# Loading the first section's weights first, and sending each token's residual with it to its expert

## The chip, the cores and the metric

The kernel runs on one core of a Trainium2 chip. A core has five engines that run their own instruction streams: TensorE (PE in the profile; PEld is its weight load), VectorE (DVE), ScalarE (ACT), GpSimd (POOL) and SyncE (SP), which here only issues transfers. Engines wait for one another and for transfers by semaphores. The metric is the device time of one execution in microseconds (us); lower is better.

## The reference, cut to what matters

The reference is a decoder of four layers with a self-attention part, a cross-attention part and a feed-forward part each, over 32 sequences of 128 tokens with 128 features (4,096 tokens). Each part normalizes the residual stream and adds its result to it. Only the last part matters for the change: a mixture of 8 experts in which every token goes to one expert.

```
h = layernorm(x)                          # 4096 x 128
e, p = argmax(h @ Wr), softmax value of it # one expert per token
place = number of earlier tokens that chose e   # dropped if place >= 512
y[token] = relu((p * h) @ W1[e]) @ W2[e]  # 128 -> 512 -> 128
out = x + y                               # dropped tokens: out = x
```

Everything ahead of it (a delta-rule layer first, then attention, gated and expert feed-forward layers, a state-space layer, L0_delta to L3_cross by the kernel's names) is computed section by section.

## The kernel before, in words

The 32 sequences are cut into groups of two (`G` = 2). Two streams of such groups, 0 and 1, are in work at once, half a round apart: while stream 0 is in its first six sections, stream 1 is in its last six, so that the engines find work in both. Strings of digits (`TURNS`, `LAST_TURNS`) say, for each engine, which stream issues its next piece; this order is fixed when the program is built. PSUM's eight banks are handed round as a ring (class `Psum`).

The program has these parts, with a barrier of all engines after each:

- Set-up (lines 461 to 528). SP and ACT issue the loads of the early weights, among them weights of later sections and constants that are staged in the streams' scratch memory. After all have landed, VectorE converts and scales (L505 to L522), and SP goes on issuing: the late weights (L471), the experts of L2_moe (L473, L477), and a transfer that writes zeros over `expert_in` in HBM (L480). The barrier waits for SP's issuing too.
- "first" (`stretch("first")`): stream 1 alone does its first six sections. Its inputs are loaded at the start (L2321 to L2324). VectorE's first piece waits for them. L0_cross waits for the late weights.
- "round", 7 times: both streams do twelve sections.
- "last": stream 0 does twelve sections, stream 1 its last six.
- The experts of L3_moe, in two rounds of 4 experts (L2462). SP loads for each expert its rows and both weights (L2528 to L2530). TensorE transposes the rows (L2470, 4 tiles of 128 tokens), multiplies up (L2475) and down (L2484). VectorE copies the result (L2522), and SP stores it to `expert_out` (L2533).
- The result, in two rounds of 16 sequences (L2548). SP loads places (L2552) and the stored residual (L2556), GpSimd gathers each token's row from `expert_out` with 16 indirect transfers (L2570), VectorE adds (L2583), SP stores `out` (L2561).

The function `moe3` (the section L3_moe inside the streams) only routes: the place of every token in `expert_in`, computed by short dependent VectorE operations, ending with L1356 (`place`) and L1358 (the row, scaled); GpSimd scatters the rows (L1367). SP's `stored` then stores the residual and the places to HBM (L2329, L2330), waits for these and the scatter, and loads the stream's next group (L2321).

## Time and profile before

| | us |
|---|---|
| median of 3 runs | 4756.86 |
| lowest and highest run | 4756.38, 4769.69 |
| profiled execution | 4767.48 |
| its span in the profile | 4765.8 |

| engine | busy, us | share |
|---|---|---|
| TensorE | 3863.3 | 81% |
| VectorE | 3144.0 | 66% |
| ScalarE | 2051.9 | 43% |
| GpSimd | 678.6 | 14% |

The profiled execution is as long as the longest of the three timed runs. Its span is the time from its first to its last recorded event. All times below count from the start of the span. By the timeline, "first" begins at 56 us, the experts of L3_moe at 4613 us and the result part at 4706 us.

### The profile page before, as it was taken

To read this page: it belongs to the slowest core of one execution; us is meant where nothing else is said; L and a number is where in the kernel's file an instruction comes from. 1 tells how busy PE (TensorE), PEld (TensorE's weight loads), DVE (VectorE), ACT (ScalarE), POOL (GpSimd) and SP (SyncE) were. 2 spreads that over 40 slices of the span, in tenths; PEclk is the share of its full clock that TensorE was granted. 3 is DMA by queue.
4 is the path that set the end of the run, shared out by engine and by line. 5 is a ranking of instruction groups with operands and counts; after the bars stand their busy time and mean duration, and the time that the engine had idled before them with its cause. 6 is when DMAs were issued, how large, how long until landed. Compare 5 with 4: busy or idle time off the path is not lost. (4 is left out here: it accounts for less than half of the span.)

```text
span 4765.8 us, 93107 instructions
## 1 busy us (share of the span) xinstructions
PE 3863.3 (81%) x36752; PEld 2707.5 (57%) x36752; DVE 3144.0 (66%) x8198; ACT 2051.9 (43%) x4873; POOL 678.6 (14%) x987
## 2 busy tenths in 40 slices
PE   1688888888878888788888888888888888889863
PEld 1456565655656565555656556565655656656642
DVE  3467767576765868677676767657686675765751
ACT  1236353454535454354534545353543535345520
POOL 1010201202020110202012020201102011120002
PEclk9679888798887988888888988879887897879886
DMA  4000000000000000000000000000000000000013
GB/s 130 1 2 1 7 2 7 2 1 7 1 7 1 6 2 1 8 1 7 2 7 2 1 7 1 7 1 6 2 1 8 1 6 2 6 2 1 1 35 91
DMA packets 69261, 45.67 MB, mean 10 GB/s; under 512 B 12995, under 2 KB 65852, under 8 KB 68590
## 3 DMA queue, kind: packets, MB, share of 16 engines
q1 hardware_dynamic: 63388, 33.03, 2.5%
q8 instruction: 303, 4.96, 0.4%
q0 software_dynamic: 2048, 3.85, 0.3%
q10 hardware_dynamic: 3378, 2.64, 0.3%
q14 instruction: 144, 1.18, 0.1%
HBM read 29.35 MB, written 10.50 MB: 8 GB/s over the span
## 5 line engine op out<-in xcount | busy, mean ns | idle before, releaser
L756 PE MATMUL banks<-scratch 32*128 32x512 f32 x2048 | 479.3, 741 | 45.3 <-DVE scratch L1741 17.6
L330 ACT ACT_TABLE_LOAD x321 | 411.8, 1283 | 13.3 <-PE banks L1083 7.8
L902 DVE TENSOR_REDUCE scratch<-banks 128x4 f32<-128x512 f32 x512 | 321.4, 681 | 76.8 <-PE banks L729 47.6
L1590 PE MATMUL banks<-scratch,w_ident 128*128 128x256 f32 x1024 | 298.8, 418 | 75.9 <-DVE scratch L1741 75.9
L1678 ACT ACTIVATE scratch<-scratch,ssm_A 128x256 f32<-128x256 f32 x512 | 231.4, 506 | 292.8 <-DVE scratch L1735 282.7
L866 ACT ACTIVATE scratch<-banks 128x512 f32<-128x512 f32 x512 | 269.9, 599 | 154.8 <-PE banks L790 154.1
L1874 PE MATMUL banks<-scratch 32*32 32x32 f32 x10496 | 274.0, 219 | 72.7 <-issue 44.8
L1735 DVE TENSOR_TENSOR_SCAN scratch<-scratch 128x512 f32<-128x512 f32 x256 | 312.9, 1222 | 15.4 <-ACT scratch L1678 8.6
L1874 PEld LDWEIGHTS banks<-scratch 32*32 32x32 f32 x10496 | 243.8, 131 | 123.4 <-issue 85.9
L581 POOL TENSOR_TENSOR 0_rstd<-0_var,minus_half 128x2 f32<-128x2 f32 x96 | 80.6, 840 | 1289.0 <-DVE 0_var L599 1079.3
L1590 PEld LDWEIGHTS banks<-scratch,w_ident 128*128 128x128 f32 x1024 | 191.9, 205 | 125.6 <-DVE scratch L1741 99.9
L806 PE MATMUL banks<-scratch 128*32 128x128 f32 x4096 | 225.1, 292 | 39.9 <-ACT scratch L866 31.0
L756 PEld LDWEIGHTS banks<-scratch 32*128 32x128 f32 x2048 | 150.7, 211 | 186.8 <-issue 50.3
L581 POOL TENSOR_TENSOR 1_rstd<-1_var,minus_half 128x2 f32<-128x2 f32 x96 | 67.6, 704 | 1297.1 <-DVE 1_var L599 1191.7
L1220 PEld LDWEIGHTS banks<-experts,scratch 128*128 128x128 f32 x1792 | 238.1, 198 | 17.7 <-issue 6.3
L1256 ACT ACTIVATE scratch<-banks,w_e_b 128x256 f32<-128x256 f32 x448 | 190.6, 473 | 133.6 <-PE banks L1212 131.4
L1220 PE MATMUL banks<-experts,scratch 128*128 128x128 f32 x1792 | 245.1, 283 | 1.5 <-DVE scratch L1741 1.2
L576 PE MATMUL banks<-w_ident,1_hn 128*128 128x128 f32 x192 | 59.9, 382 | 208.8 <-DVE 1_hn L604 208.4
L806 PE MATMUL banks<-scratch,w_slots 128*32 128x128 f32 x4096 | 222.6, 286 | 2.7 <-issue 2.7
L790 PEld LDWEIGHTS banks<-scratch,sel_part_bf 128*128 128x128 bf16 x2048 | 166.2, 107 | 89.8 <-issue 25.8
L914 DVE RECIPROCAL scratch<-banks 128x128 f32<-128x128 f32 x128 | 121.7, 951 | 143.1 <-PE banks L806 142.0
L790 PE MATMUL banks<-scratch,sel_part_bf 128*128 128x128 bf16 x2048 | 205.5, 237 | 1.5 <-ACT scratch L858 1.4
(516 smaller groups left out, 8635.3 us busy)
## 6 DMA issues: line engine op xcount, KB each, us to landing
experts<-in_e_W SPq DMA_DIRECT2D x16, 256.0 KB, 5.3
w_e_W<-in_e_W SPq DMA_DIRECT2D x3, 704.0 KB
expert_in<-scratch SPq DMA_DIRECT2D x1, 2048.0 KB, 14.1
scratch<-expert_in SPq DMA_DIRECT2D x8, 256.0 KB, 4.6
expert_out<-scratch SPq DMA_DIRECT2D x8, 256.0 KB, 2.3
scratch<-residual SPq DMA_DIRECT2D x8, 256.0 KB, 3.1
out<-scratch SPq DMA_DIRECT2D x8, 256.0 KB, 2.4
experts<-in_e_w SPq DMA_DIRECT2D x1, 1792.0 KB, 7.7
```

The source lines that it names most:

```text
L330: act.preload_act_table_set(name)
L756: last = pe.matmul(row_tiles(t), lhs[r, col(s)], rhs[r, s], start=True, stop=letter == "S" and mask is None, skip_group_check=True)
L790: last = pe.matmul(t[:, i * L:(i + 1) * L], sel_part[:, a:a + 1].broadcast_to([128, 128]), mT[:, col(s)], start=False, stop=i == NI - 1, s ...
L806: last = pe.matmul(t[32 * i:32 * i + 32, k * L:(k + 1) * L], W["slots"][:, 32 * j:32 * j + 32] if k else vslot[:, s, j, i, :], pT[:, s % 2 ...
L866: P.give(act.activation(pT[:, s % 2, j, :], t, ACT.Exp), f"{nm}.T{s}{j}")
L902: P.give(dve.tensor_reduce(negm[:, s, NI * j:NI * j + NI], row_tiles(t), X, ALU.max, negate=True), f"{nm}.S{s}{j}")
L1220: last = pe.matmul(t[:, col(s)], hid[:, e % RING, c, col(s)], w2[:, 2 * e + c, :], start=c == 0, stop=c == 1, skip_group_check=True)
L1256: P.give(act.activation(hid[:, e % RING, c, :], t, ACT.Gelu, bias=W["e2_b1"][:, 2 * e + c:2 * e + c + 1]), f"{nm}.u{e}.{c}")
L1590: last = pe.matmul(total[:, c * N:(c + 1) * N], ident[:], yc[:, k % RING, j, :], start=False, stop=n == DS - 2 and j == 1, skip_group_chec ...
L1678: ins = act.activation(decay[:, k % RING, j, :], dstart[:, c, :], ACT.Exp, scale=ssm_A[:, c, n + j:n + j + 1])
L1735: dve.tensor_tensor_scan(*flat, 0.0, ALU.mult, ALU.add).then_inc(ev(nm + ".state"), 1)
L1874: last = pe.matmul(t[dst, h * width:(h + 1) * width], lhs(h), rhs(h), start=True, stop=True, skip_group_check=True)
```

## The change

- Only the weights of L0_delta and four constants (`EARLY`) are loaded in the set-up. VectorE keeps one operation there. All other weights, the staged constants, L2_moe's experts and the zeros are issued by SP at the head of "first", behind the groups' inputs (`late_setup_sp`). VectorE's conversions and ScalarE's exponential move to the place where stream 1 comes to L0_cross; there every engine waits for them.
- A row of `expert_in` now has 257 words (`ROW`): the scaled token, its residual and its number. ScalarE copies the residual into the row, VectorE writes the number and counts it up.
- The residual is stored to `out`, and no places are stored.
- In "last", SP loads the weights of 7 of the 8 experts ahead of stream 0's store.
- The experts run in one part, without a loop. The rows are loaded in four lots. The next expert's transposes are issued ahead of the expert before it multiplied down. VectorE adds the residual while it reads PSUM, and GpSimd scatters each expert's finished rows straight to `out`, 4 indirect transfers for each expert. `expert_out`, the stored places and the result part are gone.

```diff
-LATE = ("x0_", "a1_", "m_", "e1_", "a2_", "x2_", "e2_", "s_", "e3_")
+EARLY = ("ident", "blocks", "head_of", "delta_masks")
...
-        early_loads = plain
+        early_loads, staged, plain = [], plain, []
         for name, t in dram.items():
-            plain = late_loads if name.startswith(LATE) and name not in ("s_A_log", "s_D") else early_loads
+            plain = early_loads if name.startswith("d_") or name in EARLY else late_loads
...
+        late_loads = staged + late_loads
...
-        expert_in = nc.dram_tensor("expert_in", (E3 * CAP, D), F32, kind="Internal").ap()
-        expert_out = nc.dram_tensor("expert_out", (E3 * CAP, D), F32, kind="Internal").ap()
-        res_d = nc.dram_tensor("residual", (B, L, D), F32, kind="Internal").ap()
-        place_d = nc.dram_tensor("places", (B // G, 128, G), U32, kind="Internal").ap()
+        expert_in = nc.dram_tensor("expert_in", (E3 * CAP, ROW), F32, kind="Internal").ap()
...
-                for dst, src in late_loads:
-                    sp.dma_start(dst, src).then_inc(s_late, 16)
-                if "L2_moe" in SECTIONS:
-                    sp.dma_start(experts[:, 0:E2 * F2], dram["e2_w1"]).then_inc(s_e2, 16)
-                    w2 = experts[:, E2 * F2:2 * E2 * F2].rearrange("p (c f) -> p c f", f=D)
-                    w2_d = dram["e2_w2"].rearrange("(c p) f -> p c f", p=128)
-                    for c in (slice(0, E2), slice(E2, 2 * E2)):
-                        sp.dma_start(w2[:, c], w2_d[:, c]).then_inc(s_e2, 16)
-                sp.wait_ge(s_pool, 1)
-                sp.dma_start(expert_in.rearrange("(p c) f -> p c f", p=128),
-                             spread(zeros, E3 * CAP // 128)).then_inc(s_zero, 16)
...
+                dve.tensor_tensor(mix_onorm[:], W["d_mix_w"][:], W["d_onorm_w"][:], ALU.mult).then_inc(s_setup, 1)
                 dve.wait_ge(s_setup, 2)
+        def late_setup_sp(sp):
+            for dst, src in late_loads:
+                sp.dma_start(dst, src).then_inc(s_late, 16)
+            if "L2_moe" in SECTIONS:
+                sp.dma_start(experts[:, 0:E2 * F2], dram["e2_w1"]).then_inc(s_e2, 16)
+                w2 = experts[:, E2 * F2:2 * E2 * F2].rearrange("p (c f) -> p c f", f=D)
+                w2_d = dram["e2_w2"].rearrange("(c p) f -> p c f", p=128)
+                for c in (slice(0, E2), slice(E2, 2 * E2)):
+                    sp.dma_start(w2[:, c], w2_d[:, c]).then_inc(s_e2, 16)
+            sp.dma_start(expert_in.rearrange("(p c) f -> p c f", p=128),
+                         spread(zeros, E3 * CAP // 128)).then_inc(s_zero, 16)
+        def late_setup_act(act):
+            tables.use(act, EXP)
...
+        def late_setup_dve(dve, q):
+            q.link(dve.tensor_scalar(scale3[:], W["x3_scale"][:], 1.0, None, ALU.add))
+            for n in ("gate", "up", "down"):
+                dve.tensor_scalar(fw[n][:], W["f_" + n], float(np.float32(1.0 / 127.0)), None, ALU.mult)
...
+            dve.wait_ge(s_setup, 3)
+            dve.tensor_scalar(ssm_A[:], ssm_A[:], -1.0, None, ALU.mult).then_inc(s_setup, 1)
...
+                        act.copy(rows[:, :, D:2 * D], xres[:]).then_inc(ev(nm + ".placed"), 1)
...
                         dve.tensor_copy(place[:], top).then_inc(ev(nm + ".placed"), 1)
-                        for s in range(G):
-                            dve.tensor_scalar(scaled[:, s, :], hn[:, s, :], den[:, s:s + 1], None,
+                        q.link(dve.tensor_copy(rows[:, :, 2 * D].bitcast(U32), token))
+                        dve.tensor_scalar(token, token, float(STREAMS * N), None,
+                                          ALU.add).then_inc(ev(nm + ".placed"), 1)
+                        for s in range(G):
+                            dve.tensor_scalar(rows[:, s, 0:D], hn[:, s, :], den[:, s:s + 1], None,
                                               ALU.mult).then_inc(ev(nm + ".placed"), 1)
                     def pool_f(pool, q):
                         norm_pool(pool, nm)
                         yield
-                        pool.wait_ge(ev(nm + ".placed"), G + 1)
+                        pool.wait_ge(ev(nm + ".placed"), G + 3)
                         pool.wait_ge(s_zero, 16)
                         for s in range(G):
                             pool.indirect_dma_start(
-                                expert_in, bass.IndirectOffsetOnAxis(place[:, s:s + 1], 0), scaled[:, s, :], None,
+                                expert_in, bass.IndirectOffsetOnAxis(place[:, s:s + 1], 0), rows[:, s, :], None,
...
-                    sp.wait_ge(ev(f"{u}e3.placed"), 1)
+                    if part == "last" and order == SECTIONS:
+                        sp.wait_ge(ev(f"{u}.hn"), G * norm(f"{u}s3") + 1)
+                        for v in range(STREAMS):
+                            if v != u:
+                                sp.wait_ge(ev(f"{v}e3.placed"), G + 3)
+                        for e in range(E3 - 1):
+                            load_expert3(sp, e, s_e3)
+                    sp.wait_ge(ev(f"{u}e3.placed"), G + 3)
                     sp.dma_start(r_d[g], xres[:]).then_inc(s_out, 16)
-                    sp.dma_start(l_d[g], place[:]).then_inc(s_out, 16)
                     yield
-                    sp.wait_ge(s_out, 32)
+                    sp.wait_ge(s_out, 16)
...
+                            if part == "first" and engine == 1:
+                                late_setup_act(args[0])
+                            if part == "first" and engine == 2:
+                                late_setup_dve(*args)
+                            args[0].wait_ge(s_setup, 4)
...
+        W3 = [(experts[:, 2 * e * F3:(2 * e + 1) * F3], experts[:, (2 * e + 1) * F3:(2 * e + 2) * F3])
+              for e in range(E3 - 1)] + [(S1.take(F3), S1.take(F3))]
...
+                turned(0)
+                pe.wait_ge(s_e3, 32 * (E3 - 1))
+                for e in range(E3):
+                    if e == E3 - 1:
+                        pe.wait_ge(s_last3, 32)
+                    up(e)
+                    if e + 1 < E3:
+                        turned(e + 1)
+                    if e >= 1:
+                        down(e - 1)
+                down(E3 - 1)
...
+                        ins = dve.tensor_tensor(rows_out[:, e - 1], row_tiles(t), rows_in[:, e - 1, :, D:2 * D], ALU.add)
...
+                for k, (a, b) in enumerate(lots):
+                    sp.dma_start(rows_in[:, a:b], in_d[:, a:b]).then_inc(s_rows[k], 16)
+                    if k == 1:
+                        load_expert3(sp, E3 - 1, s_last3)
+            @block.gpsimd
+            def _(pool):
+                for e in range(E3):
+                    for k, (a, _) in enumerate(lots):
+                        if e == a:
+                            pool.wait_ge(s_rows[k], 16)
+                    P.wait_given(pool, f"down{e}")
+                    for c in range(NB3):
                         pool.indirect_dma_start(
-                            taken[:, b, :], None, expert_out,
-                            bass.IndirectOffsetOnAxis(places[:, b // G, b % G:b % G + 1], 0),
-                            bounds_check=E3 * CAP - 1, oob_is_err=False).then_inc(s_taken[b // per], 16)
-                @block.vector
-                def _(dve):
-                    dve.memset(taken, 0.0).then_inc(s_clear, 1)
-                    dve.wait_ge(s_stream, 16 * pieces)
-                    for k in range(pieces):
-                        dve.wait_ge(s_taken[k], r * (16 * per) + 16 * per)
-                        b = slice(k * per, (k + 1) * per)
-                        dve.tensor_tensor(stream_in[:, b], stream_in[:, b], taken[:, b], ALU.add).then_inc(s_added, 1)
-            clear([s_places, s_stream, s_clear, s_added, s_final])
-            nc.all_engine_barrier()
+                            result, bass.IndirectOffsetOnAxis(rows_in[:, e, c, 2 * D:ROW].bitcast(U32), 0),
+                            rows_out[:, e, c, :], None, bounds_check=B * L - 1, oob_is_err=False).then_inc(s_final, 16)
+                pool.wait_ge(s_final, 16 * E3 * NB3)
```

SP in the part "last", before (numbers in brackets are semaphores waited for; `1e3.placed` is raised by L3_moe of stream 1, `rows_placed1` by its scatter):

```order
L2426 UNCONDITIONAL_BRANCH
L2329 DMA residual<-1_xres 128x2x128 [waits 1e3.placed]
L2330 DMA places<-1_place 128x2
L2329 DMA residual<-0_xres 128x2x128 [waits 0e3.placed,rows_placed1,group1_stored]
L2330 DMA places<-0_place 128x2
L2409 UNCONDITIONAL_BRANCH [waits rows_placed0,group0_stored]
```

and now:

```order
L2460 UNCONDITIONAL_BRANCH
L2347 DMA out<-1_xres 128x2x128 [waits 1e3.placed]
L2407 DMA experts<-in_e_W 128x512 [waits 0.hn,1e3.placed,rows_placed1,group1_stored]
L2408 DMA experts<-in_e_W 128x4x128
...
L2407 DMA experts<-in_e_W 128x512
L2408 DMA experts<-in_e_W 128x4x128
L2347 DMA out<-0_xres 128x2x128 [waits 0e3.placed]
L2443 UNCONDITIONAL_BRANCH [waits rows_placed0,group0_stored]
```

Fourteen loads (seven pairs) stand between the two stores, behind stream 1's scatter and ahead of stream 0's store.

VectorE in "first", at the end of L0_delta and the start of L0_cross, before:

```order
L2232 TENSOR_TENSOR scratch<-scratch 128x256 [waits 1d0.rr,dve_steps]
L610 TENSOR_TENSOR 1_xres<-1_xres,banks 128x256 [waits bank4_filled]
L671 TENSOR_SCALAR 1_mask_f<-1_mask_i 128x256 [waits context1_loaded,late_weights_loaded,bank4_emptied]
L672 TENSOR_SCALAR 1_pad_row<-1_pad_row_u 1x256
L674 CAST 1_mask_bf<-1_mask_f 128x256 [waits 1.ctx.maskf]
```

and now:

```order
L617 TENSOR_TENSOR 1_xres<-1_xres,banks 128x256 [waits bank4_filled]
L513 TENSOR_SCALAR scale<-w_x_scale 128x1 [waits late_weights_loaded,bank4_emptied]
L515 TENSOR_SCALAR fw_gate<-scratch 128x384 [waits dve_steps]
L515 TENSOR_SCALAR fw_up<-scratch 128x384
...
L527 TENSOR_SCALAR skip_diag<-w_ident,w_s_D 128x128 x2
L529 TENSOR_SCALAR ssm_A<-ssm_A 128x32 [waits setup]
L678 TENSOR_SCALAR 1_mask_f<-1_mask_i 128x256 [waits context1_loaded,setup]
L679 TENSOR_SCALAR 1_pad_row<-1_pad_row_u 1x256
```

All of VectorE's set-up but one operation now stands between the residual of L0_delta and the first operation of L0_cross.

VectorE at the end of L3_moe of stream 1 in the rounds, before:

```order
L1352 TENSOR_TENSOR scratch<-scratch 128x2 [waits dve_steps]
L1354 TENSOR_REDUCE scratch<-scratch 128x2 [waits 1.exp,dve_steps]
L1355 RECIPROCAL scratch<-scratch 128x2 [waits dve_steps]
L1356 CAST 1_place<-scratch 128x2 [waits dve_steps]
L1358 TENSOR_SCALAR scratch<-1_hn,scratch 128x128 x2
```

and now:

```order
L1362 TENSOR_REDUCE scratch<-scratch 128x2 [waits 1.exp,dve_steps]
L1363 RECIPROCAL scratch<-scratch 128x2 [waits dve_steps]
L1364 CAST 1_place<-scratch 128x2 [waits dve_steps]
L1365 CAST scratch<-w_token 128x2
L1366 TENSOR_SCALAR w_token<-w_token 128x2 [waits dve_steps]
L1369 TENSOR_SCALAR scratch<-1_hn,scratch 128x128 x2
```

Two small operations have come in ahead of the scaled rows, the second of them behind the first's result.

## Rows read from the trace of the kernel before

**Rows 1.** The page: busy time of each engine, and SP's transfer queue.

```profile
PE 3863.3 (81%) x36752; PEld 2707.5 (57%) x36752; DVE 3144.0 (66%) x8198; ACT 2051.9 (43%) x4873; POOL 678.6 (14%) x987
...
q1 hardware_dynamic: 63388, 33.03, 2.5%
```

**Rows 2.** Timeline of the start: start us, duration us, engine, line, operation, names, count [idle before].

```profile
0.75 0.41 SPq L468 DMA_DIRECT2D scratch<-in_f_gate  x1
...
13.59 0.43 SPq L468 DMA_DIRECT2D w_rope<-in_rope  x1
...
20.12 0.36 DVE L505 TENSOR_SCALAR fw_gate<-scratch 128x384 f32<-128x384 int32 x1 [20.12 <-DMA w_rope<-in_rope]
...
23.36 0.28 DVE L512 TENSOR_TENSOR mix_onorm<-w_d_mix_w,w_d_onorm_w 128x128 f32<-128x128 f32 x1
...
25.20 0.17 DVE L522 TENSOR_SCALAR ssm_A<-ssm_A 128x32 f32<-128x32 f32 x1
...
50.39 4.65 SPq L480 DMA_DIRECT2D expert_in<-scratch  x1
56.19 5.17 SPq L2321 DMA_DIRECT2D 0_xres<-in_x  x1
...
62.79 0.38 SPq L2321 DMA_DIRECT2D 1_xres<-in_x  x1
...
66.22 0.49 DVE L590 BATCH_NORM_STATS2 1_stats<-1_xres 128x6 f32<-128x128 f32 x2 [40.84 <-DMA 1_xres<-in_x]
```

**Rows 3.** Timeline of "first", from L0_delta to L0_cross on VectorE.

```profile
153.96 0.42 DVE L610 TENSOR_TENSOR 1_xres<-1_xres,banks 128x256 f32<-128x256 f32 x1 [2.47 <-PE banks L1965]
...
154.42 0.29 DVE L671 TENSOR_SCALAR 1_mask_f<-1_mask_i 128x256 f32<-128x256 int32 x1
```

**Rows 4.** Timeline of the first round, from stream 1's places to its next group.

```profile
529.44 0.17 DVE L1356 CAST 1_place<-scratch 128x2 uint32<-128x2 f32 x1
...
535.70 0.41 SPq L2321 DMA_DIRECT2D 1_xres<-in_x  x1
...
537.88 0.49 DVE L590 BATCH_NORM_STATS2 1_stats<-1_xres 128x6 f32<-128x128 f32 x2 [1.42 <-DMA 1_xres<-in_x]
```

**Rows 5.** The scatters of L1367: from issue to landing, over all 32.

```profile
DMA to landing us min/median/max: 3.1/3.5/4.4
```

**Rows 6.** DMA of the stretch 44.86 to 65 us: PE, PEld, DVE, ACT, POOL, PEclk, DMA share, GB/s.

```profile
44.86:65.00 20.14, 0.00 (x0) 0.00 (x0) 0.00 (x0) 0.00 (x0) 0.00 (x0) 1.00 1.07 319
```

**Rows 7.** Timeline of the end of "last" and the start of the experts.

```profile
4595.24 0.98 POOL L1367 DMA_INDIRECT expert_in<-scratch,1_place  x1 [0.30 <-issue]
...
4609.14 0.98 POOL L1367 DMA_INDIRECT expert_in<-scratch,0_place  x1 [0.30 <-issue]
4613.61 0.39 SPq L2528 DMA_DIRECT2D scratch<-expert_in  x1
...
4619.06 1.12 PE L2470 MATMUL banks<-w_ident,scratch 128*128 128x128 f32 x4 [14.78 <-DMA experts<-in_e_W]
```

**Rows 8.** Timeline of the first round of experts on TensorE.

```profile
4627.50 3.70 PE L2475 MATMUL banks<-scratch,experts 128*128 128x512 f32 x8 [0.68 <-ACT scratch L2510]
...
4635.88 3.70 PE L2475 MATMUL banks<-scratch,experts 128*128 128x512 f32 x8 [0.67 <-ACT scratch L2510]
...
4639.42 3.73 PE L2484 MATMUL banks<-experts,scratch 128*128 128x128 f32 x32
...
4644.26 3.70 PE L2475 MATMUL banks<-scratch,experts 128*128 128x512 f32 x8 [0.68 <-ACT scratch L2510]
...
4655.14 0.69 DVE L2522 COPY scratch<-banks 128x512 f32<-128x512 f32 x1 [2.88 <-PE banks L2484]
```

**Rows 9.** Timeline of the result part.

```profile
4750.57 0.69 DVE L2583 TENSOR_TENSOR scratch<-scratch 128x512 f32<-128x512 f32 x1 [4.44 <-DMA scratch<-expert_out,places_all]
4750.62 1.51 POOL L2570 DMA_INDIRECT scratch<-expert_out,places_all  x1 [0.31 <-issue]
...
4762.63 0.37 SPq L2561 DMA_DIRECT2D out<-scratch  x1
```

More of the change, by code:

```diff
@@ L45 @@
 CAP = B * L // E3
-LOT3 = 4
-LOTC = min(16, NGROUPS * STREAMS * G)
+ROW = 2 * D + 1
+NB3, NCH3 = CAP // 128, F3 // 128
 RING_BANKS = 8
@@ L494, in _ @@
                 pool.memset(ones_sq[:], 1.0)
-                pool.memset(zeros, 0.0).then_inc(s_pool, 1)
+                pool.memset(zeros[:, 0:2 * D], 0.0)
+                pool.memset(zeros[:, 2 * D:ROW].bitcast(U32), 2 * B * L).then_inc(s_pool, 1)
                 pool.memset(ones_row_bf[:], 1.0)
@@ new lines, in late_setup_act @@
+        def late_setup_act(act):
+            tables.use(act, EXP)
+            act.activation(ssm_A[:], W["s_A_log"][:], ACT.Exp).then_inc(s_setup, 1)
+        def late_setup_dve(dve, q):
+            q.link(dve.tensor_scalar(scale3[:], W["x3_scale"][:], 1.0, None, ALU.add))
+            for n in ("gate", "up", "down"):
+                dve.tensor_scalar(fw[n][:], W["f_" + n], float(np.float32(1.0 / 127.0)), None, ALU.mult)
+            dve.tensor_copy(sel_state[:].rearrange("p a b -> p (a b)"), W["sel_state"])
+            dve.tensor_copy(sel_part[:], W["sel_part"])
+            dve.tensor_copy(sel1[:], W["sel1"])
+            dve.tensor_copy(ident_bf[:], ident[:])
+            dve.tensor_scalar(ident_root[:], ident[:], MASK_ROOT, None, ALU.mult)
+            dve.tensor_copy(causal_bf[:], W["causal"][:])
+            dve.tensor_copy(causal_T_bf[:], W["causal_T"][:])
+            for n in ("Wq", "Wq_swap", "Wk", "Wk_swap", "Wv"):
+                w = W["x3_" + n]
+                dve.tensor_scalar(w[:], w[:], scale3[:], None, ALU.mult)
+            for c in range(2):
+                dve.tensor_scalar(skip_diag[:, c, :], ident[:], W["s_D"][:, c:c + 1], None, ALU.mult)
+            dve.wait_ge(s_setup, 3)
+            dve.tensor_scalar(ssm_A[:], ssm_A[:], -1.0, None, ALU.mult).then_inc(s_setup, 1)
@@ L1302, in moe3 @@
                     top, den, mine = S.take(G), S.take(G), S.take(G)
-                    scaled = S.take(N).rearrange("p (s f) -> p s f", s=G)
+                    rows = S.take(G * ROW).rearrange("p (s f) -> p s f", s=G)
                     def pe_f(pe):
@@ L2430, in _ @@
                             load(sp, 0)
+                        late_setup_sp(sp)
                     in_turns(turns[4], P, groups, 4, sp, g)
@@ L2434, in _ @@
                             landed(sp)
+                    if part == "first":
+                        sp.wait_ge(s_zero, 16)
             clear(turn_sems(groups))
@@ L2448, in build @@
         S = Scratch(scratches[0])
-        nch, lots = F3 // 128, range(LOT3)
-        rows_in = S.take(LOT3 * CAP).rearrange("p (i c f) -> p i c f", i=LOT3, f=D)
-        rows_out = S.take(LOT3 * CAP).rearrange("p (i c f) -> p i c f", i=LOT3, f=D)
+        rows_in = S.take(E3 * NB3 * ROW).rearrange("p (e c f) -> p e c f", e=E3, f=ROW)
         xT = S.take(2 * CAP).rearrange("p (r t) -> p r t", r=2)
-        hid = S.take(2 * nch * CAP).rearrange("p (r c t) -> p r c t", r=2, c=nch)
-        w1 = experts[:, 0:LOT3 * F3].rearrange("p (i f) -> p i f", i=LOT3)
@@ L2455, in build @@
-        w2 = experts[:, LOT3 * F3:2 * LOT3 * F3].rearrange("p (i c f) -> p i c f", i=LOT3, f=D)
-        s_lot, s_stored3 = [sem(f"expert{i}_loaded") for i in lots], sem("experts3_stored")
-        P = Psum(banks, filled, emptied)
-        w1_d = dram["e3_W1"].rearrange("p (r i f) -> r p i f", i=LOT3, f=F3)
-        w2_d = dram["e3_W2"].rearrange("(r i c p) f -> r p i c f", i=LOT3, c=nch, p=128)
-        in_d, out_d = (a.rearrange("(r i c p) f -> r p i c f", i=LOT3, c=CAP // 128, p=128)
-                       for a in (expert_in, expert_out))
@@ new lines, in build @@
+        hid = S1.take(2 * NCH3 * CAP).rearrange("p (r c t) -> p r c t", r=2, c=NCH3)
+        rows_out = S1.take(E3 * CAP).rearrange("p (e c f) -> p e c f", e=E3, f=D)
+        lots = [(0, 1), (1, 2), (2, 5), (5, E3)]
+        s_rows = [sem(f"expert_rows{k}_loaded") for k in range(len(lots))]
+        s_final = sem("result_stored")
+        in_d = expert_in.rearrange("(e c p) f -> p e c f", c=NB3, p=128)
+        result = out.rearrange("b t f -> (b t) f")
+        P = Psum(banks, filled, emptied)
```

187 lines of the change are left out of this document (67 added, 120 removed).

## The prediction

> **What bounds the kernel now.** I read the page first. No engine is full: TensorE is busy 81%, VectorE 66%, ScalarE 43% of the span [rows 1]. The rounds, from about 260 to 4300 us, are a mesh of two streams in a fixed order of pieces. The change adds little there. It works at both ends, so I read the timeline there.
>
> At the start the reader is to see SP. Its first early load is issued at 0.75 us and the last, the 25th on SP, at 13.59; VectorE converts from 20.12, when all have landed. Its set-up ends at 25.37, but SP issues until 50.39 + 4.65 = 55.04, and the barrier waits for it. The first stretch's inputs queue behind the experts and the zeros: the first of them takes 5.17 us to issue, and stream 1's arrives only at 66.22, where the first real work begins [rows 2]. So 66 us pass before any of the model is computed, and nothing lies beside them.
>
> At the end the reader is to see three stages in a row. The experts begin with a load at 4613.61, TensorE starts at 4619.06 [rows 7]. In a steady round one expert takes 4644.26 - 4635.88 = 8.38 us [rows 8], a matter of TensorE. Then the result part goes at the pace of GpSimd's indirect transfers, one each 1.3 us (0.98 busy and 0.30 idle ahead of it [rows 7]), 32 of them, with TensorE idle. The last store is issued at 4762.63 [rows 9]. From 4613.6 to 4765.8 that is 152 us.
>
> **The start, term by term.** SP issues 13 transfers in place of 25 (ScalarE 13 too). At the pitch of before, (13.59 - 0.75) / 24 = 0.535 us, the last starts at 7.2 and is issued at 7.6. A landing on a free queue takes 537.88 - 535.70 = 2.2 us [rows 4], so 9.8; the upper bound is the 6.1 us of before (20.12 - 14.02), with four times the bytes queued. VectorE's one operation (0.28 us [rows 2]) gives 10.1. From SP's last issue to the first of the next stretch it was 56.19 - 55.04 = 1.15 us, so 11.25. Stream 1's input is the fifth issue, at the pitch 0.41 + some 0.1 us [rows 4] about 1.9 us on, and lands 2.2 us later: 15.3. Against 66.22 that saves **50.9 us** (47 to 52).
>
> What is moved must be paid at L0_cross. VectorE's conversions, 20.12 to 25.37, less the one that stays and its step (0.2), are 5.05 us. They stand between 153.96 + 0.42 and 154.42 [rows 2, 3], where VectorE had no pause, and all engines now wait for them; TensorE and ScalarE, which ran ahead there, start together with VectorE afterwards, which I put at 0.3 us. So **+5.4 us** (5 to 7). The exponential runs on ScalarE beside it. Will the late weights be there? SP issues some 75 transfers from 15 us at 0.5 us each, to about 52 us, and L0_cross comes at 154.4 - 50.9 = 103. That cover is 50 us deep; VectorE's late set-up does not wait. The experts' and the zeros' bytes (3.6 and 4.2 MB at 319 GB/s [rows 6], 25 us) come last and end near 80 us, long before the scatters that need them. While they flow, the first section runs beside busy queues, which no row shows with work on the engines; I take 0 and keep 5 us for it.
>
> **The rounds.** Each of 16 passes of L3_moe gets two small VectorE operations and a ScalarE copy of 128x256. A small one costs 0.17 us [rows 4], so 0.34 at most, x16 = 5.4 us of VectorE. The copy, by the nearest row (VectorE's addition of the same size, 0.42 us [rows 3]), is x16 = 6.7 us of ScalarE, which is less than half busy. Then the chain of stream 1: place, scatter, landing, load, next group. It is open, for VectorE sat idle 1.42 us for that input [rows 4]. It grows by 0.34 us, plus what a row of 1,028 bytes takes more than one of 512 to land: 0 to 0.9 us, the spread of landings from median to worst (3.5 to 4.4 [rows 5]). Seven times that is 2 to 9 us. SP saves the stores of places, but waits for the scatter, not for them: nothing. If all was covered the sum is 0 (a gain below that has no source but the order of pieces falling better, which I bound at -10), if nothing, 5.4 + 6.7 + 9 = 21. I take **+8**: VectorE in full, as it is the one in the chain, and the low end of the load chain.
>
> **The last stretch.** Stream 1's second scatter is issued at 4595.24 and lands 3.5 us later [rows 5, 7], near 4599. Then SP issues the 14 loads, 3.67 MB, 11.5 us at 319 GB/s [rows 6]: to about 4611. Stream 0's store stands behind them and lands at some 4613.5. Before, the scatter at 4609.14 + 3.5 = 4612.6 ended the stretch. So this prefetch is hidden but for about 1 us, and the loads that follow have less to bring. At 200 GB/s it would be 6 us late; that is my bound.
>
> **The experts.** The first row load now starts near 4614.6. It brings 0.53 MB in place of 0.77, so it lands within 4.5 us (before, 4619.06 - 4613.61 = 5.45). TensorE starts at 4619 as before, and its second expert at 4627.5 as before [rows 7, 8]. From there no second load wait, and no wait for the transposed rows: 8.38 - 0.67 = 7.7 us for an expert. Seven of these and the last multiplication down (3.73 us [rows 8]): 4627.5 + 53.9 + 3.7 = 4685.1. The remaining row lots (3.2 MB to the fifth expert) need 10 us at 319 GB/s and are due after 12.
>
> VectorE's addition takes the place of its copy (0.69 us [rows 8]): for the seventh expert it ends at 4682.1, for the eighth at 4685.8. GpSimd needs 4 x 1.3 = 5.2 us for an expert against 7.7 of TensorE, so it keeps up, but the last two stand close: 4682.1 + 5.2 = 4687.3, the last transfer starts 3.9 later at 4691.2, lands after 3.5 at 4694.7; 1 us to close: 4695.7. Against 4765.8: **70.1 us** saved.
>
> What if GpSimd's issues are slower beside a busy VectorE? One took 1.51 us as VectorE's addition of two operands in SBUF ran with it [rows 9], against 0.98 alone [rows 7]. At that price for all, an expert needs 7.3 us, still under 7.7, and the end moves by 5 us at most. By the Trainium skill ("SBUF — State Buffer", "SBUF: two separate sides") VectorE shuts GpSimd out of a shared pair of ports when it reads two operands from SBUF or runs in its two-port mode, so that transfers issued by GpSimd wait for their descriptors. The trace agrees, with that 1.51. By the rule the new addition, which reads one operand from PSUM, would not block, and the sum stays; by the page's example of about 3.1 us for one blocked transfer, 32 of them would be an estimated 109 us and GpSimd the bound.
>
> **Sum.** 50.9 - 5.4 - 8 + 70.1 = 107.6 us. The profiled execution took 4767.5, so 4659.9 by its own time. It stands 10.6 above the median of the runs shown, 4756.9, and what makes that difference I don't know; the gain lies in stretches that don't depend on it. I apply the gain to the median: **4649 us**. What a measurement can tell from no change is 0.3%, 14 us.
>
> **Rivals.**
> - The rounds give half back. Their order of pieces is fixed to old durations, and a piece that comes 0.3 to 1 us late can hold the other stream too. For it: the 1.42 us idle for the load shows the chain is open [rows 4]. Against: shares of 66% and 43% leave room [rows 1]. At 6 us in each of eight passes, 48 in place of 8: 4689. Chance 0.14.
> - GpSimd or the rows' transfers set the pace at the end. At 2.5 us for an issue (1.51 plus one more blocking and the pitch's 0.3) 32 take 80 us, from the first finished expert at 4635 to 4715, closing at 4719: a gain of 47 in place of 70, 4672. It decides above 7.7 / 4 = 1.9 us. For it: the 1.51; against: VectorE's operations there read PSUM. Chance 0.08.
> - The start doesn't do what it says: the first section waits for the weights or is starved by the late ones' queue, and L0_cross starts hardly earlier. Half of 45.5 lost: 4672. Against: 50 us of cover. Chance 0.03.
> - Slower than before: a row of 257 words moves word by word. SP's queue took 2.5% of 16 engines' span for 63,388 packets [rows 1], 0.03 us each; 128 rows x 257 words are 32,896 packets, over 16 engines 62 us, two for a group. Seven open load chains are then some 860 us longer, about 5500. It decides from 107.6 / 7 = 15 us more for a landing. Against: the row is one contiguous run on both sides. Chance 0.04.
>
> **How the numbers follow.** Forecast 0.71, the others 0.29. The forecast's own range is 4630 to 4668: rounds -10 to +21 around +8, start and end some 6 us each, and the 10.6 us between runs. The range to hold 8 in 10 reaches on to the third and part of the second case: 4630 to 4682. Faster has all but the last case and a remainder, 0.94; the same 0.02; slower 0.04.
>
> **What would show it.** In the new profile: the first normalization of stream 1 at 14 to 17 us (L597); about 5.5 us of VectorE set-up ahead of L678, without idle for a load; the rounds' period within 1 us of before; row loads issued 1 to 2 us after the second scatter lands; a TensorE period of 7.5 to 7.8 us over eight experts; indirect transfers 1.3 us apart and 4 to an expert. I would be wrong if the rounds' period had grown by more than 3 us, if TensorE waited among the experts, or if landings of scatters exceeded 5 us.

## The result and the profile after

| | before | changed |
|---|---|---|
| median of the runs on one chip, us | 4756.62 (4749.41 to 4769.69, 4 runs) | 4639.33 (4630.15 to 4647.79, 4 runs) |
| profiled execution, us | 4767.5 | 4647.79 |
| its span, us | 4765.8 | 4645.7 |

The medians differ by 117.3 us. The ratio, 0.9769 with a 95% interval of 0.9746 to 0.9791, is not the quotient of the medians; by it the gain is 110 us (99 to 121). Forecast were 107.6 (4649, range 4630 to 4682).

The page after. TensorE runs as many matmuls as before, busy for 15 us less [rows 1]:

```profile
PE 3848.0 (83%) x36752; PEld 2703.1 (58%) x36752; DVE 3140.8 (68%) x8220; ACT 2056.2 (44%) x4889; POOL 678.2 (15%) x988
```

Its DMA queues (packets, MB, share of 16 engines). q0 carries GpSimd's indirect transfers, q8 the engines' own instructions, a queue that will matter below:

```profile
q1 hardware_dynamic: 48076, 33.04, 2.6%
q8 instruction: 304, 4.98, 0.5%
q0 software_dynamic: 2560, 5.79, 0.3%
```

The timeline of the start (start us, duration us, engine, line, what, count, [idle before <- what ended it]). Stream 1's input lands 51.4 us earlier than at 66.22 [rows 2]:

```profile
9.40 0.29 DVE L490 TENSOR_TENSOR mix_onorm<-w_d_mix_w,w_d_onorm_w 128x128 f32<-128x128 f32 x1 [9.40 <-DMA w_head_of<-in_head_of]
...
12.50 0.38 SPq L2331 DMA_DIRECT2D 1_xres<-in_x  x1
...
14.81 0.49 DVE L597 BATCH_NORM_STATS2 1_stats<-1_xres 128x6 f32<-128x128 f32 x2 [5.12 <-DMA 1_xres<-in_x]
```

The timeline of L0_cross, where the late set-up stands between two rows that were neighbours [rows 3]. It costs 5.1 us:

```profile
106.11 0.42 DVE L617 TENSOR_TENSOR 1_xres<-1_xres,banks 128x256 f32<-128x256 f32 x1 [2.46 <-PE banks L1976]
106.56 0.15 DVE L513 TENSOR_SCALAR scale<-w_x_scale 128x1 f32<-128x1 f32 x1
...
111.44 0.17 DVE L529 TENSOR_SCALAR ssm_A<-ssm_A 128x32 f32<-128x32 f32 x1
...
111.64 0.31 ACT L659 ACTIVATE scratch<-1_ctx_tok 128x128 f32<-128x128 f32 x1 [6.71 <-DVE ssm_A L529]
111.64 0.29 DVE L678 TENSOR_SCALAR 1_mask_f<-1_mask_i 128x256 f32<-128x256 int32 x1
...
115.55 0.49 DVE L597 BATCH_NORM_STATS2 1_stats<-1_xres 128x6 f32<-128x128 f32 x2 [0.99 <-ACT 1_ctxnT L673]
```

The timeline of one load chain in the rounds [rows 4]. The load is issued 3.43 us after the second scatter:

```profile
1053.20 0.97 POOL L1378 DMA_INDIRECT expert_in<-scratch,1_place  x1 [0.30 <-issue]
...
1056.63 0.38 SPq L2331 DMA_DIRECT2D 1_xres<-in_x  x1
...
1058.87 0.49 DVE L597 BATCH_NORM_STATS2 1_stats<-1_xres 128x6 f32<-128x128 f32 x2 [1.74 <-DMA 1_xres<-in_x]
```

The timeline of the end, from the last scatter of L3_moe. Three stages in a row [rows 7 to 9] have become one: TensorE goes on every 7.45 us (7.44 from 4607.72 to 4615.16), and GpSimd scatters each expert's four blocks beside it, 1.28 us apart:

```profile
4560.47 0.97 POOL L1378 DMA_INDIRECT expert_in<-scratch,0_place  x1 [0.30 <-issue]
4564.97 1.09 SPq L2573 DMA_DIRECT2D scratch<-expert_in  x2
...
4568.88 1.11 PE L2505 MATMUL banks<-w_ident,scratch 128*128 128x128 f32 x4 [13.52 <-DMA scratch<-expert_in]
...
4607.72 3.60 PE L2512 MATMUL banks<-scratch,experts 128*128 128x512 f32 x8
...
4615.16 3.60 PE L2512 MATMUL banks<-scratch,experts 128*128 128x512 f32 x8
...
4633.39 0.69 DVE L2567 TENSOR_TENSOR scratch<-banks,scratch 128x512 f32<-128x512 f32 x1 [2.58 <-PE banks L2521]
...
4640.54 0.97 POOL L2585 DMA_INDIRECT out<-scratch  x1 [0.30 <-issue]
```

The spans differ by 120.1 us. By place:

| stretch | before | after | saved |
|---|---|---|---|
| to the first norm | 66.22 | 14.81 | 51.4 |
| from there to L0_cross' residual | 87.74 | 91.30 | -3.6 |
| from there to its norm | 4.34 | 9.44 | -5.1 |
| from there to the last scatter of L3_moe | 4450.8 | 4444.9 | 5.9 |
| from there to the end | 156.7 | 85.2 | 71.4 |

### The profile page after: what moved, and what is told of

It reads as the page before. It is cut to its first block and busy times, and to the rows that moved or that the text cites. A ratio compares the mean times of both kernels' runs of the same rounds, so it can differ in the third digit from the quotient of the medians.

```text
span 4645.7 us, 92881 instructions
## 1 busy us (share of the span) xinstructions
PE 3848.0 (83%) x36752; PEld 2703.1 (58%) x36752; DVE 3140.8 (68%) x8220; ACT 2056.2 (44%) x4889; POOL 678.2 (15%) x988
## 5 line engine op out<-in xcount | busy, mean ns | idle before, releaser
L1885 PE MATMUL banks<-scratch 32*32 32x32 f32 x10496 | 276.9, 220 | 75.1 <-issue 47.3
L1885 PEld LDWEIGHTS banks<-scratch 32*32 32x32 f32 x10496 | 246.8, 132 | 125.2 <-issue 88.2
L1752 DVE TENSOR_TENSOR scratch<-scratch,banks 128x512 f32<-128x512 f32 x256 | 177.7, 694 | 19.4 <-PE banks L1616 13.8
## 6 DMA issues: line engine op xcount, KB each, us to landing
experts<-in_e_w SPq DMA_DIRECT2D x2, 896.0 KB, 14.1
```

What stands on the lines that cost most here:

```text
L1885: last = pe.matmul(t[dst, h * width:(h + 1) * width], lhs(h), rhs(h), start=True, stop=True, skip_group_check=True)
```

## The experiments

All times are medians of three or more runs, where not said otherwise, beside runs of the kernel before on the same chip (4751.8 to 4754.6 us); "end" is the time from the last scatter of L3_moe to the end of the span, "body" from L0_cross' norm to that scatter.

**The start alone.** The kernel before with the changed start (edit: only the parts of the diff in the first block, at L0_cross and in the first stretch).

> The kernel before with the changed start alone: 13 early loads on SP, the late loads, the experts and the zeros issued inside the first stretch, VectorE's and ScalarE's late set-up at L0_cross. Rounds, rows and everything after the last stretch are those of before. Theory (the start gives its own share): first norm of stream 1 at 14.8 us, a set-up of 5.1 us at L0_cross, one TensorE pause of 4.8 us where the experts' loads flow; 51.4 - 3.6 - 5.1 = 42.7 saved, about 4714 us. Rival (the two profiles' 6 us gained in the rounds come with the start): about 4708. Rival (start does nothing once the rounds have settled): 4757.

Measured: 4709.3 us, ratio 0.9912 (0.9892 to 0.9932), 45.3 saved where 42.7 follows from the trace. That fits the theory; the first rival (some 49 saved) lies 3 us off too, and an interval of 10 us on either side doesn't part them. The first norm stands at 14.49, L0_cross' norm at 115.60; the end takes 156.1 us as before.

**Rows and end alone.** The kernel before with all else of the diff, and the old start.

> The kernel before with the changed rows, stores, last stretch and experts, and the old start. Theory of the forecast (rounds +8, end 71.4 saved): 4693 us. Rival 1 (the row format costs nothing in the rounds): 4685. Rival 2 (the row format is what gained about 6 us in the rounds of the two profiles): 4679. In the profile the time from the last scatter of the last stretch to the end should be 85 us against 157 before in all three.

Measured: 4698.7 us, 0.9884 (0.9863 to 0.9906): 55.8 saved, less than any theory gave. The end takes 85.3 us as expected. What was missed lies at the start: the first norm comes at 80.27 in place of 66.22, since the zeros, which stand ahead of the inputs there, are now twice the bytes. Their transfer before and in this kernel (KB, median us to landing):

```profile
expert_in<-scratch SPq DMA_DIRECT2D x1, 2048.0 KB, 14.1
```

```profile
expert_in<-scratch SPq DMA_DIRECT2D x1, 4112.0 KB, 29.4
```

So 71.4 - 14.1 = 57.3 follows from the trace. In the changed kernel the two parts meet: the new start puts the doubled zeros behind the inputs, where they delay no input.

**Doses in the rounds.** Extra VectorE copies of the token numbers in each of 16 passes of L3_moe (14, then 28), and seven extra ScalarE copies of the residual:

```diff
+for _ in range(28):      # second dose; the first adds 14 of the same
+    q.link(dve.tensor_copy(rows[:, :, 2 * D].bitcast(U32), token))
 q.link(dve.tensor_copy(rows[:, :, 2 * D].bitcast(U32), token))
```

```diff
+for k in range(7):
+    act.copy(spare[:, k], xres[:])
 act.copy(rows[:, :, D:2 * D], xres[:]).then_inc(ev(nm + ".placed"), 1)
```

> The changed kernel, with VectorE's copy of the token numbers made 14 times more in each of the 16 passes of L3_moe (15 in place of 1, each waiting for the one before). Each takes 0.16 us and the step to the next some 0.05, so 14 x 0.21 = 2.9 us more a pass, 47 us over 16. Theory of the forecast (VectorE's operations count in full, since it is in the chain of the load): 4639 + 47 = 4686 us or more. Rival (VectorE has slack there in both streams, so the two operations of the change cost nothing): 4639, and not over 4650. Between: the passes of one stream count and those of the other don't, 4662.

> The changed kernel, with ScalarE's copy of the residual made 8 times in place of once in each of the 16 passes of L3_moe (7 x 0.39 = 2.7 us more, 44 us over 16). Theory of the forecast (ScalarE's copy is covered): 4639 us, at most 4650. Rival (it stands before the scatter or before the other stream's work): up to 4683; if for one stream alone, about 4661.

> As dose_dve, with 28 extra copies a pass in place of 14: 28 x 0.203 = 5.7 us more of VectorE a pass, 11.4 a round. The first dose left the rounds at 557.4 us, though TensorE was not busy for 4.5 us more of each: its busy time fell by as much, at a granted clock of 0.860. Theory (the clock gives back what TensorE idles): TensorE's idle time rises by another 5 us or more a round, its busy time falls again, the round stays under 560, total 4655 + 16 = 4671 us. Rival (the first dose used up what there was to give back): rounds of 563 us or more, total 4700 or more.

Measured: 4655.4 us, 4665.3 us and 4716.2 us. Six rounds of each, between loads of stream 1's input, are one row (us, then busy us of PE, PEld, DVE, ACT and POOL, PEclk, DMA share, GB/s). The changed kernel, the first dose and the second:

```profile
496.70:3844.80 3348.10, 2826.99 (x27275) 1982.67 (x27275) 2335.41 (x6133) 1537.01 (x3654) 481.93 (x709) 0.85 0.01 4
```

```profile
502.40:3847.10 3344.70, 2798.56 (x27275) 1958.39 (x27275) 2362.66 (x6300) 1536.31 (x3654) 480.96 (x708) 0.86 0.01 4
```

```profile
500.10:3901.80 3401.70, 2830.28 (x27276) 1983.21 (x27276) 2391.02 (x6467) 1534.82 (x3654) 481.21 (x708) 0.86 0.01 4
```

By six, and by the same row of other kernels:

| kernel | one round, us | TensorE busy | not busy |
|---|---|---|---|
| before | 558.6 | 473.0 | 85.6 |
| start alone | 556.4 | 470.3 | 86.2 |
| changed | 558.0 | 471.2 | 86.9 |
| rows and end alone | 557.4 | 471.8 | 85.7 |
| first VectorE dose | 557.4 | 466.4 | 91.0 |
| second VectorE dose | 567.0 | 471.7 | 95.2 |
| ScalarE dose | 560.8 | 473.8 | 87.0 |
| row format alone | 560.8 | 473.3 | 87.4 |

TensorE's pauses ("not busy") are the steadier measure. The doses put 5.7 and 11.4 us more on VectorE a round (0.203 us each), and the pauses grew by 4.2 and 8.4 us against the changed kernel, nearly three quarters; against the seven kernels with new rows, new end and no dose besides it (85.7 to 86.5) it is more, 0.8 to 0.9. So VectorE's work there is not covered. In time the first dose cost 16 of its 45 us, between its two theories, the second 77 of 91. The theory of the second dose fell: that the first left the round's length alone (TensorE was busy for 5 us less, at a granted clock of 0.86) did not repeat, and the second took 9.5 us a round more than the first. ScalarE's dose, 5.4 us a round, left the pauses alone, but the whole run was 26 us longer, and all four runs took 4664 to 4669 us, where at most 4650 were expected of a covered copy. So it is not shown that ScalarE's copies are free. TensorE was busy for 2.6 us more a round, and the granted clock is lower in this kernel's four runs (0.839 to 0.846 against 0.848 to 0.854 in the changed kernel); whether the dose or chance lowered it stays open.

**The row format alone.** The kernel before, with L3_moe's rows of 257 words and nothing else; its stores of residual and places wait until the row is complete:

```diff
-sp.wait_ge(ev(f"{u}e3.placed"), 1)
+sp.wait_ge(ev(f"{u}e3.placed"), G + 3)
```

> The kernel before with the row format alone: L3_moe writes rows of 257 words (VectorE's two small operations, ScalarE's copy, longer scatters); the old stores, start, experts and result part stay. At the start the zeros are 4.2 MB in place of 2.1: at 319 GB/s 6.6 us more. Theory of the forecast (+8 in the rounds): 4754 + 6.6 + 8 = 4769 us, rounds 1 us longer each. Rival (the rounds cover it): 4761, rounds as before (557.5 us at a granted clock of 0.85, TensorE not busy for 85.8 us of each).

Measured: 4794.1 us, 1.0085 (1.0064 to 1.0107), 42.3 us slower than before, more than either theory gave. 16.6 of these are the start (first norm at 82.80, behind the doubled zeros), 3 the end. The other 23 are left for the rounds; in the profile the body is 11 us longer and one round 2.2. The load chain shows a cause:

```profile
1112.38 0.98 POOL L1375 DMA_INDIRECT expert_in<-scratch,1_place  x1 [0.30 <-issue]
...
1117.58 0.40 SPq L2329 DMA_DIRECT2D 1_xres<-in_x  x1
```

5.20 us from the second scatter to the load. Over six rounds the mean is 5.40, in the kernel before 3.68 and with the start alone 3.36, in the changed kernel 3.11 and with rows and end alone 2.99. VectorE idles 3.65 us in each round for this input (1.9 before, 1.4 changed). SP waits for the places first, then for the scatter (us in total, times, longest; from 600 to 3900 us, the kernel before and this one):

```profile
SPq L2334 <- DMA places<-1_place: 16.0, 6, 2.8
SPq L2321 <- DMA expert_in<-scratch,1_place: 13.3, 6, 2.6
```

```profile
SPq L2342 <- DMA places<-1_place: 19.8, 5, 4.2
SPq L2329 <- DMA expert_in<-scratch,1_place: 11.6, 5, 3.1
```

In both the scatter ends the wait, 2.2 and 2.3 us behind the places. So wide rows beside a store of places land about 2 us later, and wide rows without that store a little sooner than narrow ones with it. My edit also moved both stores closer to the scatters; how much of the 2 us is that, and how much the rows, stays open.

**The loads behind L0_delta.** SP issues the second section's experts and the zeros after the late set-up:

```diff
+sp.wait_ge(s_setup, 4)
 sp.dma_start(experts[:, 0:E2 * F2], dram["e2_w1"]).then_inc(s_e2, 16)
```

> The changed kernel, but SP issues the second section's experts (3.6 MB) and the zeros (4.2 MB) only when VectorE's late set-up at L0_cross is done. Theory (TensorE's instructions are themselves fetched by transfers, and the fetch stood behind these loads): the pause of 4.79 us before L1885 at 64.57 falls to about 1.1, L0_cross begins 3.7 us earlier (its residual at 102.4 in place of 106.11), and q8's share in that stretch is small; a pause of the same kind may appear after 107 us where the loads now flow. Total within 4 us of the changed kernel, which this measurement alone can't tell. Rival (the pause comes of the clock, or of the engine's own fetch pace): the pause stays at 4.8 us.

Measured: 4632.4 us, 0.9737 (0.9709 to 0.9764). TensorE's timeline in the changed kernel, where the loads of L502 and L503 flow from 54 to 90 us:

```profile
54.28 7.80 SPq L502 DMA_DIRECT2D experts<-in_e_w  x2
...
62.12 4.93 SPq L503 DMA_DIRECT2D expert_in<-scratch  x1
64.57 2.55 PEld L1885 LDWEIGHTS banks<-scratch 32*32 32x32 f32 x123 [4.93 <-issue]
64.57 2.69 PE L1885 MATMUL banks<-scratch 32*32 32x32 f32 x123 [4.79 <-issue]
```

and in this kernel:

```profile
61.05 2.69 PE L1886 MATMUL banks<-scratch 32*32 32x32 f32 x123 [1.05 <-issue]
```

L0_cross' residual stands at 102.58, as the theory has it. TensorE's pauses of over 1 us of this kind in L0_delta sum to 4.3 to 5.0 us in the five kernels without these loads beside the 32x32 multiplications (the kernel before, rows and end alone, the row format alone, this one, three_edits below), but to 7.1 to 13.5 us in the nine with them, 8.3 in the changed one. The section, from its norm to its residual, takes 87.6 to 87.9 us in the five and 90.1 to 97.1, mean 92.4, in the nine: the 3.6 us of the changed kernel's profile are one draw, the mean is 4.6. The clock is not the cause: over this section it is granted at 0.56 both in the changed kernel and in this one. Nor did a new pause come up where the loads flow now, beside L0_cross. In three_edits they flow from 79 us on, still in L0_delta but behind its 32x32 multiplications, and cost nothing there. No engine and no load of data ends the pause; "issue" is all the trace says. That it is the fetch of TensorE's instructions fits the load of many short ones (L1885, 32x32), and q8; it is argued, that the bulk loads make it is shown. The Trainium skill ("Runtime: NRT & Kernel Launch", "Instruction fetch mechanics") says that a sequencer fetches its next instructions through a DMA queue of its own, mostly hidden. If the pause is such a fetch, it was not hidden here, beside loads at a DMA share of 1.0; no run shows the fetch itself.

**No prefetch.** The 14 loads of the experts' weights stand behind the first row load:

```diff
-for e in range(E3 - 1):
-    load_expert3(sp, e, s_e3)      # in the last stretch
+                                   # the same two lines behind the first row load
```

> The changed kernel, but the 14 loads of the weights of experts 0 to 6 (3.67 MB) are issued behind the first row load, after the last stretch, in place of during it. Theory: they need 11.5 us at 319 GB/s before TensorE may begin, against 4 us for the rows alone, so the experts begin 8 to 9 us later, and stream 0's store before them goes 1 us earlier: the time from the last scatter of L3_moe to the end 93 us in place of 85, total 4647. Rival (the prefetch is worth all 11.5 us and more, since row lots 2 to 4 now stand behind the weights and TensorE waits for them too): 100 us or more. Rival (the rows are the bound anyway): 86.

Measured: 4648.5 us, 0.9774 (0.9752 to 0.9795); the end takes 94.5 us, 9.3 more, where 8 were expected.

**The order of the transposes.**

```diff
-    up(e)
-    if e + 1 < E3:
-        turned(e + 1)
+    turned(e)
+    up(e)
```

> The changed kernel, with each expert's transposes right ahead of its multiplication up, as in the kernel before, in place of one expert ahead. Theory (TensorE then waits for ScalarE's copy of the transposed rows at each expert): the period rises from 7.45 to 8.3 us, the experts take 7 x 0.9 = 6 us more, 91 us from the last scatter of L3_moe to the end in place of 85.2. Rival (the faster period comes of the loads alone): 7.45 and 85.

Measured: 4656.5 us in one run. The end takes 90.6 us, and the period is 8.38 us, the very one of before [rows 8]:

```profile
4589.61 3.70 PE L2512 MATMUL banks<-scratch,experts 128*128 128x512 f32 x8 [0.68 <-ACT scratch L2555]
...
4597.99 3.70 PE L2512 MATMUL banks<-scratch,experts 128*128 128x512 f32 x8 [0.68 <-ACT scratch L2555]
```

TensorE then waits 0.68 us for ScalarE's copy ahead of each multiplication up. The shorter period comes of the order alone, not of the loads.

**Two operands from SBUF beside the scatters.** Six more additions behind those of experts 1 to 5:

```diff
+other = rows_out[:, e - 1] if e <= 3 else row_tiles(t)     # SBUF, or PSUM
+ins = dve.tensor_tensor(spare, other, rows_in[:, e - 1, :, D:2 * D], ALU.add)
```

> The changed kernel with six more additions of 128x512 on VectorE, written to a spare tile, behind the addition of experts 1 to 5, while GpSimd issues that expert's four scatters. For experts 1 and 2 they read two operands in SBUF, for 3, 4 and 5 one of the two is in PSUM. Theory (VectorE keeps GpSimd from issuing only while it reads two operands from SBUF): the eight scatters of experts 1 and 2 take 1.3 to 1.6 us each in place of 0.97, those of 3 to 5 stay at 0.97. Rival 1 (any busy VectorE slows them): all twenty lengthen. Rival 2 (the single issue of 1.51 us in the kernel before was chance): all stay at 0.97.

Measured: 4648.0 us in one run. GpSimd's timeline, expert 2 (other operand in SBUF) and expert 3 (in PSUM), each with VectorE busy beside it:

```profile
4602.52 1.44 POOL L2599 DMA_INDIRECT out<-scratch  x1 [1.82 <-DVE scratch L2576]
4604.27 1.15 POOL L2599 DMA_INDIRECT out<-scratch  x1 [0.30 <-issue]
4605.72 1.15 POOL L2599 DMA_INDIRECT out<-scratch  x1 [0.30 <-issue]
4607.17 0.97 POOL L2599 DMA_INDIRECT out<-scratch  x1 [0.30 <-issue]
4609.90 0.97 POOL L2599 DMA_INDIRECT out<-scratch  x1 [1.76 <-DVE scratch L2576]
4611.18 0.97 POOL L2599 DMA_INDIRECT out<-scratch  x1 [0.30 <-issue]
```

Only issues beside reads of two SBUF operands lengthen, three of four at both experts, by 0.18 to 0.47 us (1.3 to 1.6 us each were expected, 1.15 to 1.44 came); the fourth falls behind the additions. The twelve of experts 3 to 5 stay at 0.97. The theory holds in kind. The rule is that of the Trainium skill ("SBUF — State Buffer", "SBUF: two separate sides"), and the trace agrees with it, with a size well below that page's example of some 3.1 us, which is of a copy.

**Three edits to the changed kernel.** VectorE's late set-up moves into its idle time behind L0_delta's features, SP issues experts and zeros at that point, and each expert's multiplication down, addition and scatters go in halves:

```diff
 dve.tensor_scalar(feat[:, :, 8:14, :], ...).then_inc(ev(nm + ".feat"), 1)
+if part == "first":
+    dve.wait_ge(s_late, 16 * len(late_loads))
+    late_setup_dve(dve, q)
...
+sp.wait_ge(ev("1d0.feat"), 1)
 sp.dma_start(experts[:, 0:E2 * F2], dram["e2_w1"]).then_inc(s_e2, 16)
...
+for half in range(2):
+    t = P.open(pe, f"down{e}.{half}", width=CAP // 2)
```

> The changed kernel with three edits: VectorE's late set-up stands in its idle time of 11.3 us behind the features of L0_delta (only the negation of 0.17 us stays at L0_cross); SP issues the experts and the zeros at that point too; each expert's multiplication down, addition and scatters go in two halves. Theory: -4.7 us at L0_cross, -3.7 us for TensorE's pause, and -2.9 us at the end, where GpSimd's last eight scatters begin with the first half of the seventh expert: 4639 - 11 = 4628 us. Rival (the set-up delays GpSimd's or ScalarE's part of the section, or the halves cost TensorE time): 4636 or more.

Measured: 4628.0 us, 0.9731 (0.9711 to 0.9751), the lowest median of all. That it is the theory's number to the us is luck, with an interval of 10 us on either side. The timeline at L0_cross:

```profile
102.24 0.42 DVE L621 TENSOR_TENSOR 1_xres<-1_xres,banks 128x256 f32<-128x256 f32 x1 [2.46 <-PE banks L1980]
102.70 0.18 DVE L533 TENSOR_SCALAR ssm_A<-ssm_A 128x32 f32<-128x32 f32 x1
...
106.82 0.49 DVE L601 BATCH_NORM_STATS2 1_stats<-1_xres 128x6 f32<-128x128 f32 x2 [0.99 <-ACT 1_ctxnT L677]
```

The norm comes 8.7 us earlier than in the changed kernel, the end takes 83.3 us, 1.9 less (2.9 expected). The intervals of the ratios overlap a little (up to 0.9751 here, from 0.9746 there), so the 11 us between the medians are not proved; the two places are read from the trace.

**The first input ahead of the weights.**

```diff
+first_input[0](sp)      # xres of stream 1, ahead of the weights
 for dst, src in queues[0]:
     sp.dma_start(dst, src).then_inc(s_weights, 16)
```

> three_edits, and the first group's input of stream 1 is issued as SP's very first transfer, ahead of the weights, in place of behind the barrier. Theory: the first norm starts at 11.4 us in place of 14.8, since the input has landed when the first stretch begins; 4628 - 3.4 = 4625 us. Rival (another transfer, or the clock's rounds of 3 us more or less, hide it): 4628 and a first norm at 14.

What ran is not what this says: by a slip the edit was laid on the kernel with the six extra additions, not on three_edits. So it tells of the input alone. Its load is SP's first transfer, and the first norm starts at 11.22 in place of 14.81 (11.4 was expected). 4631.7 us, 0.9747 (0.9725 to 0.9769). The combination with the three edits was not run.

## Why the prediction was right, point by point

- **The start, 50.9.** 51.4. Pitch, landing and barrier held; the weights had landed at 9.40, and the load itself at 14.81, where 15.3 was put.
- **The late set-up, +5.4.** 5.1, without idle for a load, as the forecast said; the moved set-up of three_edits shows that it stood on the path.
- **The first section beside busy queues, 0 with 5 kept.** 3.6, wrongly put at nothing; over the nine kernels with these loads in that place it is 2.3 to 9.4, mean 4.6. In the changed kernel it is one pause of TensorE beside the experts' and the zeros' bytes; with these held back it is gone.
- **The rounds, +8.** This is the term that was mis-sized: they cost about nothing. By the medians, 117.3 - (51.4 - 3.6 - 5.1 + 71.4) = 3.2 us were gained where 8 were to be lost; by the ratio's 110 us, 4 were lost. One such figure has an interval of some 10 us on either side and settles nothing. Five other kernels with the new rows, the new end, no dose and more than one run give, by medians in the same way, from 1.5 lost to 4 gained; the mean of all six is 1.6 gained (they share some runs of the kernel before). The body in the profiles says neither: eight kernels with new rows and new end have 4434.6 to 4446.3, mean 4441.0, the two with the old rows and the old end 4450.8 and 4427.0, mean 4438.9. Two steps stand against each other. The doses show that VectorE's part was rightly called uncovered, at some 0.7 to 0.9 of its time in TensorE's pauses. The step "SP saves the stores of places, but waits for the scatter, not for them: nothing" is right on the wait and failed on the price: from scatter to load it takes 3.11 us in place of 3.68 (3.36 with the start alone), and with wide rows and the store 5.40. So the store that nothing waited for last made the scatter itself land later. That wide rows were no dearer because that store went fits these numbers; wide rows with the store at its old place were not run. ScalarE's share of the term, which was put at nothing, stays open.
- **The last stretch, 1 us.** 4.50 us from the last scatter to the first row load (4564.97 - 4560.47), against 4.47 [rows 7]; the prefetch is hidden.
- **Experts and end, 70.1.** 71.4. The period is 7.45 us, not 7.7, a little below the 7.5 to 7.8 that were to show it; the prefetch is worth 9.3 us of it and the order of the transposes 5.4 by their own runs, and the rest is the result part that went. All 32 issues stay near 0.97, since the addition reads PSUM, and an issue lengthens beside two operands in SBUF alone.
- **The rivals.** Not one of them happened. Half given back in the rounds: no, but the row format alone shows that its ground was real, a chain 1.7 us longer, with the added operations, goes with rounds 2.2 us longer in the profile. GpSimd as the bound: only for the last eight scatters. Rows moved word by word: no, the load follows after 3.1 us.
- **The sum** came out 9.7 us below the medians' difference: +0.5 the start, +0.3 the set-up, -3.6 the pause, +1.3 the end, and 11.2 the rounds (9.6 by the mean of the six kernels). By the ratio it is 2.3 us below. The mechanism at both ends was right; that the total came so near is in part luck, since a cost put at nothing and a cost put too high stand against each other.

## What to carry to other kernels

A transfer that nothing waits for can still be dear: by what queues behind it on its queue (the second 2 MB of zeros at the old start: 14 us) and beside an engine that works through many short instructions (2.3 to 9.4 us). Issue it where its neighbours are idle. When a stage's stores are changed, count what no longer lands beside the chain as well as what it carries more, and test a format and a store that goes with it both together and apart. And price the noise first: here a profile's rounds of one program differ by as much as a term of the sum.

## What the runs showed of the hardware

Rounds of one kernel, the same instructions each time, take 552.4 to 566.4 us. TensorE's clock is what differs. Three rounds of the kernel before, in a row:

```profile
1655.10:2212.30 557.20, 469.24 (x4547) 327.07 (x4547) 389.04 (x1019) 255.75 (x607) 80.80 (x120) 0.86 0.01 4
2212.30:2764.70 552.40, 466.10 (x4546) 326.47 (x4546) 387.57 (x1018) 254.75 (x607) 79.82 (x118) 0.87 0.01 4
2764.70:3331.10 566.40, 480.18 (x4546) 336.96 (x4546) 389.05 (x1019) 256.05 (x607) 80.22 (x119) 0.83 0.01 4
```

Between the last two TensorE is busy for 14.1 us more, the round is 14.0 us longer, and the granted clock falls from 0.87 to 0.83; VectorE and ScalarE are busy within 1.5 us of the same. It also goes with the time of whole runs: of the eleven runs of the kernel before that stand beside the last experiments, the four quickest (4740 to 4745 us) show 0.850 to 0.855, the five slowest (4756 to 4765 us) 0.843 to 0.846. The pauses of TensorE, which stay within 84 to 88 us in the kernel before, are the better thing to compare.
